# A shifted-window transformer block on one core: casts for two of the four high parts of the MLP's inner layer, and the second pair's logits placed ahead of the first product of the maxima

## The reference

```python
y = roll(ln(x, norm1_g, norm1_b), (-3, -3))            # then 8 x 8 windows of 49 tokens
q, k, v = split(windows(y) @ qkv_w.T + qkv_b)          # 16 heads of 8
attn = (q * 8 ** -0.5) @ k.T + bias[head] + mask[window]
o = softmax(attn) @ v                                  # per window and head, 49 x 49
x = x + roll(windows_back(o @ proj_w.T + proj_b), (3, 3))
h = gelu(ln(x, norm2_g, norm2_b) @ fc1_w.T + fc1_b)    # inner layer of 512
out = x + h @ fc2_w.T + fc2_b
```

## Time and profile before

| | |
|---|---|
| time, median of 3 runs | 4022.6 us (4018.7 to 4024.35) |
| the profiled execution: its own time | 4022.66 us |
| the profiled execution: span from first to last instruction | 4020.9 us |
| outside the span | 1.8 us |
| busy TensorE / VectorE / GpSimd / ScalarE | 93% / 79% / 71% / 70% |
| mean granted TensorE clock | 0.996 of full |

### The profile page before, as it was taken

One profiled execution on the slowest core, in us unless ns is written; L12 is line 12 of the kernel. 1 busy time (PEld: TensorE's weight loads), 2 busy tenths in 40 slices (PEclk: granted clock), 3 DMA queues, 4 the chain that ended last, 5 costly groups with the idle time before them and its releaser, 6 DMA issues. The chain is left out here.

```text
span 4020.9 us, 177003 instructions
## 1 busy us (share of the span) xinstructions
PE 3755.1 (93%) x75664; PEld 2949.1 (73%) x75664; DVE 3181.1 (79%) x7840; ACT 2799.1 (70%) x3840; POOL 2851.6 (71%) x3988
## 2 busy tenths in 40 slices
PE   3899999999999999999999999999999999999998
PEld 1677777777777777777777777777777777777776
DVE  6788878878888878877888888888887888788775
ACT  1677777767777777776777777777777777777774
POOL 5577767777777776777777677777777777777775
PEclk9999999999999999999999999999999999999999
DMA  2333333333333333333333333333333333333332
GB/s 78 103 112 114 115 110 111 115 107 113 116 112 112 114 111 111 111 117 108 112 117 112 112 114 113 112 114 112 112 111 114 111 112 114 113 109 112 114 107 61
DMA packets 609604, 442.02 MB, mean 110 GB/s; under 512 B 142083, under 2 KB 608371, under 8 KB 608819
## 3 DMA queue, kind: packets, MB, share of 16 engines
q1 hardware_dynamic: 608355, 428.88, 36.0%
q0 software_dynamic: 464, 1.81, 0.1%
HBM read 106.14 MB, written 51.46 MB: 39 GB/s over the span
## 5 line engine op out<-in xcount | busy, mean ns | idle before, releaser
L589 DVE TENSOR_REDUCE neg_max<-ps 113x16 f32<-113x784 f32 x1024 | 999.4, 976 | 571.0 <-PE ps L752 473.9
L411 ACT ACTIVATE probs<-ps 113x784 f32<-113x784 f32 x1024 | 843.7, 824 | 755.0 <-PE ps L787 680.4
L380 POOL TENSOR_TENSOR hid_lo<-probs,hid_hi 128x784 f16<-128x784 f32 x512 | 847.8, 1680 | 122.6 <-DVE hid_hi L582 122.4
L752 PE MATMUL ps<-mx_k,mx_q 128*49 128x196 f16 x8192 | 544.0, 253 | 168.5 <-DVE x L684 147.6
L787 PE MATMUL ps<-st_q,st_k 128*49 128x196 f16 x8192 | 697.0, 249 | 0.0
L782 PE MATMUL ps<-bias,eye_k 106*64 106x392 f16 x4096 | 687.3, 331 | 0.0
L787 PEld LDWEIGHTS ps<-st_q,st_k 128*49 128x49 f16 x8192 | 449.3, 105 | 120.9 <-issue 0.5
L582 DVE TENSOR_REDUCE hid_hi<-probs 128x784 f16<-128x784 f32 x512 | 483.0, 964 | 63.4 <-ACT probs L426 59.8
L426 ACT ACTIVATE probs<-ps,col 128x784 f32<-128x784 f32 x512 | 467.6, 913 | 89.3 <-PE ps L816 59.9
L834 PE MATMUL ps<-w_hi,hid_hi 128*112 128x128 f16 x3584 | 523.0, 226 | 2.9 <-DVE hid_hi L582 2.0
L752 PEld LDWEIGHTS ps<-mx_k,mx_q 128*49 128x49 f16 x8192 | 313.8, 103 | 259.8 <-DMA mx_q<-q_hi 129.4
(11 more groups left out here) (118 smaller groups left out, 7976.4 us busy)
## 6 DMA issues: line engine op xcount, KB each, us to landing
st_k<-k_hi SPq DMA_DIRECT2D x256, 196.0 KB
st_q<-q_hi SPq DMA_DIRECT2D x1024, 49.0 KB
oT_raw<-pv_sb SPq DMA_DIRECT2D x256, 196.0 KB, 3.5
x_in<-in_x SPq DMA_DIRECT2D x224, 196.0 KB
x_res<-in_x SPq DMA_DIRECT2D x224, 196.0 KB
out_y<-y_out SPq DMA_DIRECT2D x224, 196.0 KB
mx_k<-k_hi SPq DMA_DIRECT2D x512, 49.0 KB
mx_q<-q_hi SPq DMA_DIRECT2D x128, 196.0 KB
```

The lines of the kernel that those rows point to most:

```text
L380: nc.gpsimd.tensor_tensor(hid_lo[:, c, :], hid[:, c, :], hid_hi[:, c, :], ALU.subtract).then_inc(s_hid_lo, 1)
L411: nc.scalar.activation(probs[0:KP, w % 4, :].rearrange("p (b c) -> p b c", b=2), ps[0:KP, b:b + 2, 0:HB * WT], ACT.Exp).then_inc(s_exp, 1)
L589: nc.vector.tensor_reduce(neg_max[0:KP, :, :, w].rearrange("p e g -> p g e"), ps[0:KP, 0:2, :].rearrange("p b (g c) -> p (b g) c", g=2)[:, ...
L752: last = mm(group(im, 0, g, 256), mx_q[edge(n)][:, g, span], mx_k[:, g, :, span], start=True, stop=True)
```

## The change

Two edits. First, `hid_high` for chunks 2 and 3 is written as a copy (which converts float32 to float16) where it was a reduction; chunks 0 and 1 stay. Second, TensorE's program has the exact logits of pair 1 directly behind those of pair 0, ahead of `max_logits(t + 1, 0)`. Nothing else moves: no DMA, no semaphore, no count of a semaphore.

```diff
@@ VectorE
+                if c < 2:
+                    last = nc.vector.tensor_reduce(hid_hi[:, c, :], hid[:, c, :].unsqueeze(2), AX_X, ALU.max)
+                else:
+                    last = nc.vector.tensor_copy(hid_hi[:, c, :], hid[:, c, :])
+                last.then_inc(s_hid_hi, 1)
-                nc.vector.tensor_reduce(hid_hi[:, c, :], hid[:, c, :].unsqueeze(2), AX_X,
-                                        ALU.max).then_inc(s_hid_hi, 1)
@@ TensorE
                 for w in range(NW):
                     if exists(t):
-                        logits(t, w, edge, odd(0))
+                        if w != 1:
+                            logits(t, w, edge, odd(0))
+                        if w == 0:
+                            logits(t, 1, edge, odd(0))
                         if w % 2 == 0 and w > 0:
                             pv(t, w // 2 - 1)
```

## The result

The changed kernel takes 3953.0 us (median of 4 runs, 3943.86 to 3954.99) against 4020.87 us before (4 runs): ratio 0.9824, 95% interval 0.981 to 0.9839, so 68 us or 1.8% faster. The forecast was 3920, with 0.70 on 3905 to 3940 and 8 in 10 on 3900 to 3980. The profiled execution took 3954.99 us, span 3953.2.

What follows compares the result with a forecast made beforehand. TensorE's program, stalled each turn at the first product of the maxima by VectorE's x1, bounds the kernel. The second product comes 0.82 us earlier; 125 turns make 102 us off 4022.66: 3920 us, range 3905 to 3940 (0.70).

Steps and rivals of the forecast that it cites:

- What bounds the kernel: TensorE's first product of the maxima waits for VectorE's x1 in about 125 turns; 120 such waits total 147.6 us.
- The casts: On VectorE, two reductions of 0.964 us become casts of 0.568, saving 0.79 us before x1, less 0.09 for GpSimd.
- The sign that I had named: On GpSimd, hid_lo of chunk 2 was to start behind both of VectorE's casts.
- The slower rival: hid_lo of chunk 2 on GpSimd comes between the casts; 0.50 us lost a turn, 62 us, 4085 us; chance 0.08.
- The sum for casts alone: Casts alone put the first product of the maxima near 2014.25, winning 0.56 us a turn, 70 us.
- The order on TensorE: Two logits blocks in a row from 2012.70 leave TensorE ready for the first product of the maxima at 2014.18.
- The failed step: mx_q's transfer on SyncE's queue doesn't move, 2.29 us from issue to product; 0.10 us put on the first product's mean.
- The rival of the late transfer: mx_q's transfer decides the first product through SyncE's queue phase; only 0.37 us won a turn, 46 us, 3976 us; chance 0.08.
- The range: Total time: 3905 to 3940 us with 0.70; 3900 to 3980, reaching to the transfer's case, 8 times in 10.
- What is late next: TensorE's second product of the maxima waits about 0.5 us for the row maxima, 1.66 us behind the first; before 1.95.
- By parts: Each edit's share on TensorE's turn: order alone 0.29 us, 36 us; casts alone 0.56 us, 70 us.
- The held copies of the set-up: Two 128-element SBUF copies, started at 20.61, lasted until 35.43 while GpSimd ran memsets: a cast can be held likewise.

Runs made afterwards that it cites:

- the four casts: Both edits, with the high parts of chunks 0 and 1 written as casts too, against the changed kernel: 4032.07 us, 79 us more.
- x_in's load later: Both edits, with SyncE issuing the load of x_in behind mx_q instead of near its turn's head, against the changed kernel: 3932.23 us, 21 us less.
- the logits ahead: Both edits, with the exact logits one pair earlier through the whole loop, against the changed kernel: 3932.3 us, 21 us less.

## Why the prediction was right and where it was wrong

**What bounds the kernel.** Right: 125 turns with one wait each at the first product; changing what stands ahead of it moved the time, and what follows gave next to nothing back (the second product comes 0.60 us earlier in the mean, the turn is 0.58 us shorter). SyncE's wait for the end of the attention, 4.65 us a turn before, is 493.0 / 127 = 3.88 us, where 3.8 was forecast.

**The casts.** Right in mechanism and size. x1 ends 2.93 us behind the projection's start in the mean (2013.96 - 2010.99 = 2.97 forecast). The casts take 602 ns in the mean, not 568: the first of them is over 600 ns in 19 of 128 turns, those in which hid_lo of chunk 1 ran on. The race between the second cast and GpSimd went VectorE's way in 127 of 128 turns (once that cast took 1.92 us). The sign that I had named, hid_lo of chunk 2 starting behind both casts, isn't what the rows show: it starts while the second cast runs and is longer, 1.94 us in the mean for 1.68. The slower rival's mechanism exists, as the four casts show, but this place is hardly open to it. The sum for casts alone was 70 us, measured 67.

**The order on TensorE.** TensorE is ready at 3.11 us behind the projection's start, 0.08 better than the 3.19 that I had, since I counted a change of product after both blocks.

**The failed step is mx_q.** "It doesn't move, as it hangs on SyncE's queue": its issue doesn't (0.68 and 0.66 us), its landing does, from 2.33 to 2.66 us behind the issue. The 0.10 us that I put on the mean was 0.40 (3.51 against 3.11): 0.12 of it is the queue's phase (3.23 with every landing at 2.33), about as priced, and 0.28 the late landings, which the sum had at nothing. In the rows of before 2.3 us held at nearly every turn (111 of 122) because the instruction fetches fell elsewhere: in 122 turns only 2 of those on queue 8 started 1 to 3 us behind the projection's start. The edit moves a block of logits to just there, and the fetches with it; the runs with only one edit show that the order does it and the casts don't. The rival of the late transfer (3976 us) had the right place and the wrong reason: it took the queue's phase for the cause. The one late turn in the rows that I had, 1.45 us of phase, was no sample of it. The turn at 1705, where TensorE waits for mx_q in the kernel before, would have been: 3.4 us from issue to product at an ordinary phase.

```profile
1706.18 0.60 SPq L282 DMA_DIRECT2D mx_q<-q_hi  x1
```

```profile
1709.55 0.53 PE L752 MATMUL ps<-mx_k,mx_q 128*49 128x196 f16 x8 [1.32 <-DMA mx_q<-q_hi]
```

**The range.** 3953 us lies outside the 3905 to 3940 that had 0.70, and inside 3900 to 3980 only because that was stretched to the transfer's rival. That the wide range held is not a merit of the sum: the rival that stretched it had another cause.

**What is late next.** Right: 1.66 us from the first to the second product forecast, 1.67 measured in the mean, and 51.6 us of waits where 40 to 70 were named.

**By parts.** The order alone was put at 36 us and gave 19, for the same reason. Both parts together won less than their sum (68 against 86), because with both, x1 no longer hides the late landings: with the order alone they move the first product by 0.12 us in the mean (3.94 against 3.82), with both by 0.28. The difference, 0.16 us x 125 = 20 us, is about the 18 that are missing.

**The ports that VectorE and GpSimd share.** The Trainium skill (SBUF — State Buffer, section Who interferes with whom) says that a cast in its two-port form and GpSimd exclude each other for the whole instruction, by the order of issue. Here the traces agree: 2.30 us for a cast that came 0.21 us too late, 3.58 for the pair of GpSimd's operations of which the first came while the cast ran. The held copies of the set-up, which waited through several memsets, go beyond it.

## What to carry to other kernels

When an edit removes the last arrival of several, look at how each of the others is distributed over the turns, not at its usual value: the second-last had a tail that the last one hid. A transfer on which TensorE waits should be issued with two or three microseconds to spare (the delays here go up to 2.3), because an instruction fetch can fall on it and comes where the program puts it, so that moving code can make a transfer late that it doesn't touch. A wait filled by moving work is only gone if the place that the work came from doesn't open: count the blocks and the gaps.

## What the runs showed of the hardware

- An instruction fetch (16 KB, 1.17 us) costs nearly nothing in the span's shares (1.1% of the engines' time) and yet set the time of a third of the turns, as one sixteenth of a 196 KB transfer lands up to 2.3 us behind the others; in the late turn shown 4.11 us behind the projection's start for the last part, at most 2.50 for the others. The delay is longer than the fetch: the last part lands about 1.45 us behind the fetch's recorded end. Why it is so long, no run here tells. That the fetches which moved are TensorE's is argued from their number (58 and 58) and from the two runs with one edit each; the records don't name the engine.
- TensorE's idle times without a named releaser (20 over 0.15 us in the change, 10.7 us, most of them ahead of the product with v) all end 1.2 to 1.6 us behind the end of a 16 KB fetch, the same lag; in the kernel before it is all 16 (9.1 us). Such stretches behind fetches cover 6% of the span, so that this is no accident. It looks as if TensorE waited there for its own instructions, which no run tests. They are rarer in the runs with x_in's load later and with the logits ahead (4 and 2 times), and why stays open.
- A VectorE cast held by GpSimd took over at the end of GpSimd's running operation, 0.43 us ahead of its own end, and GpSimd's next operation was held in its turn. In the set-up, copies of the same kind were held through a run of memsets. Why the one hands over and the other doesn't, no run here tells.
- A DMA issue costs 0.54 us on ScalarE's queue and 0.60 on SyncE's for the same transfer.
